# Layernorm stage of a graph layer: the groups overlap on VectorE, tables and weights are moved, two batches are gathered ahead of the barrier

## The reference, cut to what matters

```python
xn = _layernorm(x, axis=-1)                  # x: 6250 x 256, float32
msg = jax.nn.relu(xn[src] + edge_attr)       # 106250 edges, 256 channels
agg = jnp.zeros_like(xn).at[dst].add(msg)    # dst is sorted
h = xn + agg                                 # then an MLP with norms over all nodes
...
qkv = xn @ W_qkv + b_qkv                     # mixing part: q and k centred over channels
attn = v + t2
mix = attn @ W_out + b_out
...
x = x + gnn(xn, ...) + mix
x = x + experts(_layernorm(x))               # top 2 of 8 experts
```

## Time and profile before

| what | us |
|---|---|
| median of 3 runs | 2200.09 |
| lowest and highest run | 2200.0, 2203.48 |
| the profiled execution, its own time | 2199.33 |
| span of the profiled execution | 2197.5 |
| barrier at the end of the layernorm stage (first DVE instruction behind it) | 83.49 |
| last gather of the edge stage issued | 1147.74 |

### The profile page before, as it was taken

One profiled execution on the slowest core, in us unless ns is written; L12 is line 12 of the kernel. 1 busy time (PEld: TensorE's weight loads), 2 busy tenths in 40 slices (PEclk: granted clock), 3 DMA queues, 4 the chain that ended last, 5 costly groups with the idle time before them and its releaser, 6 DMA issues. The chain is left out here.

```text
span 2197.5 us, 33446 instructions
## 1 busy us (share of the span) xinstructions
PE 1781.7 (81%) x10022; PEld 1420.9 (65%) x10023; DVE 1188.2 (54%) x2750; ACT 803.8 (37%) x1624; POOL 1155.5 (53%) x1121
## 2 busy tenths in 40 slices
PE   4267777777778889988886989675899999999996
PEld 3255555555555556655555878564688888888885
DVE  7354554554545555555553767769444544454443
ACT  4133232332323333333322567330344444444443
POOL 1577777777777777777760000220344444444443
PEclk8688888888878898888887999668899999999998
DMA  7566666666666676676652646776123222322332
GB/s 250 184 208 216 214 227 211 219 222 210 225 207 222 220 238 227 225 237 223 226 191 84 220 151 224 203 245 230 36 48 48 43 44 48 48 43 44 48 48 30
DMA packets 142023, 356.34 MB, mean 162 GB/s; under 512 B 33130, under 2 KB 79625, under 8 KB 127611
## 3 DMA queue, kind: packets, MB, share of 16 engines
q0 software_dynamic: 66624, 157.12, 26.9%
q1 hardware_dynamic: 69068, 198.31, 26.2%
q10 hardware_dynamic: 6255, 0.10, 0.3%
HBM read 297.49 MB, written 57.94 MB: 162 GB/s over the span
## 5 line engine op out<-in xcount | busy, mean ns | idle before, releaser
L190 POOL DMA_INDIRECT gathered<-xn_rows,src_table x832 | 821.6, 988 | 260.4 <-issue 252.8
L816 PE MATMUL bank<-edge_attr,dst_select 128*128 128x256 f32 x1664 | 534.0, 492 | 229.0 <-DVE node_sum L642 171.7
L816 PEld LDWEIGHTS bank<-edge_attr,dst_select 128*128 128x128 f32 x1664 | 411.6, 253 | 347.7 <-ACT edge_attr L730 212.2
L630 DVE TENSOR_TENSOR edge_attr<-gathered,edge_attr 128x512 f32<-128x512 f32 x416 | 260.8, 688 | 468.0 <-DMA gathered<-xn_rows,src_table 464.4
L730 ACT ACTIVATE edge_attr<-edge_attr 128x2048 f32<-128x2048 f32 x104 | 198.7, 1910 | 732.7 <-DVE edge_attr L630 732.7
L1797 PE MATMUL bank<-rowsT_parts,expert_weights 128*128 128x256 f16 x3564 | 409.4, 274 | 10.0 <-issue 6.3
L1797 PEld LDWEIGHTS bank<-rowsT_parts,expert_weights 128*128 x3564 | 346.8, 98 | 59.0 <-issue 18.0
L1758 POOL DMA_INDIRECT out<-expert_out,output_row_of_slot x108 | 183.4, 1698 | 301.2 <-ACTq L1856 278.8
L1903 DVE SCALAR_TENSOR_TENSOR gated<-bank,silu 128x512 f32<-128x512 f32 x216 | 120.6, 558 | 184.9 <-ACT silu L1842 173.7
L1810 PE MATMUL bank<-expert_weights,gated_parts 128*128 x1836 | 209.3, 273 | 0.4 <-DVE gated_parts L1911 0.4
L1810 PEld LDWEIGHTS bank<-expert_weights,gated_parts 128*128 128x128 f16 x1836 | 179.5, 98 | 21.5 <-issue 0.7
(11 more groups left out here) (274 smaller groups left out, 1883.4 us busy)
## 6 DMA issues: line engine op xcount, KB each, us to landing
edge_attr<-in_edge_attr SPq DMA_DIRECT2D x104, 1024.0 KB
raw_weights<-in_L_ffn_w SPq DMA_DIRECT2D x32, 544.0 KB, 4.6
expert_weight_parts<-weight_parts SPq DMA_DIRECT2D x32, 544.0 KB, 3.1
expert_weights<-expert_weight_parts SPq DMA_DIRECT2D x8, 2176.0 KB, 24.4
gathered<-xn_rows,src_table POOLq DMA_INDIRECT x832, 3.2
rows_in<-xn_rows SPq DMA_DIRECT2D x48, 128.0 KB
rows_in<-in_x SPq DMA_DIRECT2D x48, 128.0 KB
residual_rows<-key SPq DMA_DIRECT2D x48, 128.0 KB, 2.3
```

The lines of the kernel that those rows point to most:

```text
L190: pool.indirect_dma_start(out=rows[:, e, :], out_offset=None, in_=k.xn_d[:, :], in_offset=bass.IndirectOffsetOnAxis(ap=k.src[:, b, e:e + 1 ...
L630: last = dve.tensor_tensor(ea[:, e:e + ADDED, :], ga[:, e:e + ADDED, :], ea[:, e:e + ADDED, :], ALU.add)
L816: last = pe.matmul(WINP[j % 2][:, 0:C], SEL[j % 3][:, e, :], EA[j % 3][:, e, :], start=e == 0, stop=e == EK - 1)
```

## The change

In the layernorm stage:

- VectorE's `norm` is cut in two. `spread(n)` takes the statistics and merges them; `norm(n)` does the rest. The order is spread(0), spread(1), norm(0), spread(2), norm(1), and so on: the statistics of the next group stand ahead of the normalization of this one.
- Of the tables, only the src table is made between groups: `src_floats` ahead of norm(1), `src_columns` ahead of norm(3). `dst_floats`, `centred`, `bases`, `turned_weights`, `locals_` and `products` follow norm(6).
- TensorE turns the src table behind group 0, and the rest behind group 6.
- ScalarE copies the transposed group n-1 (`turned_rows`) between the square root and the normalization of group n.
- POOL stores all groups, gathers batch 0, waits for the dst table to do its one select, and gathers batch 1, all ahead of the barrier. The loop of the edge stage starts at batch 2.

The number of instructions on VectorE, ScalarE and POOL is as before. The diff, cut to its core:

```diff
@@ scalar
+            for n in range(NG):
+                h = n % 2
+                act.wait_ge(var_done, n + 1)
+                act.activation(std[h][:, :], mv[h][:, :, 1], ACT.Sqrt, bias=k.eps[:, :]).then_inc(std_done, 1)
+                if n >= 1:
+                    turned_rows(n - 1)
+                act.wait_ge(scale_done, n + 1)
+                act.wait_ge(blank, 1)
...
+                last.then_inc(xn_act, 1)
+            turned_rows(NG - 1)
@@ gpsimd
-            for n in range(5):
-                store(n)
-            pool.wait_ge(dst_local, 1)
-            pool.affine_select(out=k.dstl[:, NB - 1, :], in_=k.dstl[:, NB - 1, :], compare_op=ALU.is_ge, fill=0.5,
-                               base=-SEEN, pattern=[[1, EK]], channel_multiplier=EK).then_inc(seen_out, 1)
-            for n in range(5, NG):
+            for n in range(NG):
                 store(n)
             pool.wait_ge(src_ready, 2)
             pool.wait_ge(xn_st, 16 * (NG + 1))
             gather(k, pool, 0, k.GA[0], k.g_in[0])
+            pool.wait_ge(dst_local, 1)
+            pool.affine_select(out=k.dstl[:, NB - 1, :], in_=k.dstl[:, NB - 1, :], compare_op=ALU.is_ge, fill=0.5,
+                               base=-SEEN, pattern=[[1, EK]], channel_multiplier=EK).then_inc(seen_out, 1)
+            gather(k, pool, 1, k.GA[1], k.g_in[1])
@@ vector
-            for n, work in enumerate((None, table_floats, bases, centred, turned_weights, locals_, products)):
+            spread(0)
+            for n in range(NG):
+                if n + 1 < NG:
+                    spread(n + 1)
+                if n == 1:
+                    src_floats()
+                if n == 3:
+                    src_columns()
                 norm(n)
-                if work:
-                    work()
+            for work in (dst_floats, centred, bases, turned_weights, locals_, products):
+                work()
@@ tensor
-            for n, work in enumerate((None, table_turns, base_rows, None, weight_products, None, None)):
+            for n in range(NG):
                 turn(n)
-                if work:
-                    work()
+                if n == 0:
+                    table_turns(srcf, 6, src_turned, 1)
+            table_turns(dstf, 4, dst_turned, 2)
+            base_rows()
+            weight_products()
@@ edge stage, gpsimd
-            for b in range(1, NB):
+            for b in range(2, NB):
```

More of the change, by code:

```diff
@@ L278, in _, with turned_rows @@
             act.wait_ge(k.consts, k.CONST)
[L279 to L289, removed]
+            def turned_rows(n):
                 for s, (g, w) in enumerate(STEPS):
@@ L299, in _ @@
                                        bank[m % BANKS][:, 0:C].rearrange("p (b n) -> p b n", b=CB)[:, :, 0:v], ACT.Copy).then_inc(tr_free, 1)
+            for n in range(NG):
[6 more added lines that the diff above has]
+                act.wait_ge(blank, 1)
+                for g in range(G - ON_ACT, G):
+                    v = valid(n, g)
+                    last = act.activation(k.UTn[0:v, tile(n, g), :], X[n % NX_BUF][0:v, g, :], ACT.Identity,
+                                          scale=rstd[h][0:v, g:g + 1], bias=nmr[h][0:v, g:g + 1])
+                last.then_inc(xn_act, 1)
+            turned_rows(NG - 1)
         @block.gpsimd
@@ L335, in _, with spread @@
             gather(k, pool, 0, k.GA[0], k.g_in[0])
+            pool.wait_ge(dst_local, 1)
+            pool.affine_select(out=k.dstl[:, NB - 1, :], in_=k.dstl[:, NB - 1, :], compare_op=ALU.is_ge, fill=0.5,
+                               base=-SEEN, pattern=[[1, EK]], channel_multiplier=EK).then_inc(seen_out, 1)
+            gather(k, pool, 1, k.GA[1], k.g_in[1])
         @block.vector
         def _(dve):
-            def norm(n):
+            def spread(n):
                 h, x = n % 2, X[n % NX_BUF]
@@ L344, in norm @@
                 dve.drain()
-                if n > 1:
-                    dve.wait_ge(std_done, n - 1)
-                    dve.wait_ge(xn_act, n - 1)
                 for g in range(G):
@@ L351, in norm @@
                 dve.sem_inc(var_done, 1)
+            def norm(n):
+                h, x = n % 2, X[n % NX_BUF]
                 dve.wait_ge(k.consts, k.CONST)
                 dve.wait_ge(std_done, n + 1)
+                if n > 1:
+                    dve.wait_ge(xn_act, n - 1)
                 dve.reciprocal(rstd[h][:, :], std[h][:, :])
@@ L360, in norm, with src_floats, src_columns, dst_floats @@
                 last.then_inc(xn_dve, 1)
-            def table_floats():
+            def src_floats():
                 dve.wait_ge(tab_in, 16 * 6)
+                dve.tensor_copy(srcf[:, :], srci[:, :]).then_inc(tab_f, 1)
+            def src_columns():
+                dve.wait_ge(src_turned, 1)
+                for j in range(2):
+                    dve.tensor_copy(k.src[:, :, 4 * j:4 * j + 4].rearrange("p b k -> p k b"),
+                                    bank[6 + j][:, 0:4 * NB].rearrange("p (k b) -> p k b", k=4)).then_inc(src_ready, 1)
+            def dst_floats():
                 dve.tensor_copy(dstf[:, :], dsti[:, :]).then_inc(tab_f, 1)
-                dve.tensor_copy(srcf[:, :], srci[:, :]).then_inc(tab_f, 1)
             def bases():
@@ L378, in bases @@
                 dve.tensor_copy(basef[0:1, 1, :], basei[0:1, 1, :]).then_inc(base_ready, 1)
[L379 to L382, removed]
             def centred():
@@ L460, in turn, with table_turns @@
                     last.then_inc(tr_full, 1)
[L462 to L468, removed]
+            def table_turns(rows, at, done, count):
+                pe.wait_ge(tab_f, count)
+                for e in range(EK):
+                    last = pe.transpose(bank[at + e // 4][:, (e % 4) * NB:(e % 4 + 1) * NB],
+                                        rows[:, :].rearrange("b (p k) -> b k p", k=EK)[:, e, :], k.ident[0:NB, 0:NB])
+                last.then_inc(done, 1)
             def base_rows():
```

## The result

| | before | after |
|---|---|---|
| median of 20 runs, us | 2204.57 | 2198.48 |
| lowest and highest run | 2199.01, 2208.07 | 2194.81, 2201.46 |
| the profiled execution, its own time | 2199.33 | 2194.86 |
| its first gather | 70.92 | 62.54 |
| its first gather of batch 2 | 95.56 | 86.98 |

The ratio is 0.9976 with a 95% interval of [0.9969, 0.9983]: faster by 5.3 us (3.7 to 6.8); the two medians of the table lie 6.1 us apart. Forecast were 11.0 us. The direction was right, the size twice what came. 2198.48 also lies above the range, partly since the median of before stood at 2204.57 in these runs and not at the 2200.09 I started from; by the ratio, the 2200.09 would have become some 2194.8, inside the range and near rival 2.

The account below looks back on a forecast made before the run. POOL's gather issue sets the edge stage's pace, so the first gather's start counts: 12.8 us earlier, less 0.8 for the select and 1.0 for contention, 11.0 in all. From 2200.1 that gives 2189.1 us, range 2182 to 2196.

Parts of the forecast that it names:

- rival 2: Loads of x as slow as before's median, 8.7 us: 4.2 us later, 2193.3 us; chance 0.16.
- load 3: Layernorm stage, group 3's x: issued at 14.4 behind other loads, 7.0 MB in all, landing at 23.0, read at 23.3.
- load 6: Layernorm stage, last group's x: issued at 35.0 in two pieces, landing at 41.2.
- VectorE's tail: Tables and weights behind the last group, beside POOL's gathers: ends at 79.0, POOL's batch 1 at 79.6.
- the sum: First gather 12.8 us earlier, less 0.8 for the select, less 1.0 for contention: 11.0 us gained.
- the select: Between batches 0 and 1: POOL doesn't wait for the dst table and pays about 0.8 us for select and issue.
- contention: Gathers of batches 0 and 1 slowed by VectorE's work beside them: 1.0 us, bounds 0 and 8.3.
- ScalarE ended 3.0 us behind VectorE: Last group: ScalarE copies group 5's transposes ahead of its tiles, ending at 51.8, VectorE at 48.5.
- Rival 3: Contention at its bound, 8.3 us instead of 1.0: 2196.4 us; chance 0.06.
- rival 4: Gathers move but nothing follows, POOL spending the 11 us in waits on adding: 2199.5 us; chance 0.06.
- rival 1: Loads faster than taken, VectorE the chain throughout: group 6 ends 5.8 us earlier, 2183.3 us; chance 0.14.
- rival 5: Shorter prefetch turns on itself, loads 4 and 6 adding their lateness in full: slower than before, chance 0.03.

Follow-up runs that it names:

- c3: Changed kernel with POOL holding back the stores of groups 3 and 4 until group 6's x has landed; ratio 0.9964.
- d1: Changed kernel with the 106-row piece of x's last load issued as 96 and 10 rows; ratio 0.9908.
- c0: The kernel before, run again unchanged for a second trace; 2200.18 us.
- c1: The changed kernel, run again without edits; 2193.41 us, ratio 0.9971.
- c2: The changed kernel, run once more without edits on the same chip as c1; 2193.40 us, ratio 0.9972.
- b4: Changed kernel with five x buffers, ScalarE's last tiles ahead of group 5's copies, and weights' loads behind all x loads; 2184.25 us, ratio 0.9921.
- b3: Changed kernel with the weights' loads issued behind all loads of x; ratio 0.9954.
- a1: Changed kernel with five buffers for x instead of three, two of them the gather buffers; ratio 0.9934.
- c's chip: The chip shared by the runs c0, c1, c2 and c3; the kernel before took 2200.18 us there.
- d2: Changed kernel with the last store's 106 rows, not the load's, issued as 96 and 10; ratio 0.9951.
- b2: Changed kernel with batch 1 gathered behind the barrier again, leaving only the layernorm stage's change; ratio 0.9996.

## Why the prediction was half right

| step | forecast | after |
|---|---|---|
| load 2 landed | 15.1 | 15.05 |
| norm(1) ended | 20.7 | 20.9 |
| load 3 landed | 23.3 | 24.9 |
| norm(2) ended | 28.0 | 29.9 |
| norm(4) ended | 39.3 | 41.1 |
| load 6: issued, landed | 35.0, 41.2 | 36.6, 45.5 |
| norm(5) ended | 46.0 | 50.5 |
| VectorE, ScalarE done with group 6 | 48.5, 51.8 | 53.0, 56.0 |
| last store issued | 52.4 | 56.6 |
| first gather | 58.1 | 62.5 |
| VectorE's tail, POOL's batch 1 ended | 79.0, 79.6 | 82.0, 83.2 |
| first gather of batch 2 | 82.9 | 87.0 |

**The step that failed** is the landing of the loads, and load 6 above all. Of the 4.4 us at the first gather, 1.6 came from load 3, and 2.6 from load 6, which took 8.9 us where I gave it 6.2. Everything behind, up to the first gather, carried them along nearly unchanged.

For load 3 the rates were near (288 GB/s to 20 us and 355 to 25 us in the changed kernel, against 295 and 374). At these rates the 7.0 MB of the forecast's count would have passed by 23.5 instead of 23.0; by 24.93, when VectorE began on the load, 7.5 MB had. So the larger part of the error is 0.5 MB that the count leaves out. The second store, issued at 21.43, ran beside load 3 and would fill it; no run tests that. For load 6 the choice of row was wrong. The earlier trace rows give the shortest of six loads of 896 KB in one DMA. Load 6 isn't one of them; it is two DMAs, one of 106 rows, and I took a whole load's duration for it, and the shortest at that. The trace of before had the answer in its stretches, which the prediction did not use. Load 6 was issued at 35.27 and 35.69 in it, and the same slow tail stands behind the fast part:

```profile
41.00:42.00 1.00, 0.00 (x0) 0.00 (x0) 0.86 (x7) 0.00 (x0) 0.00 (x0) 1.00 0.86 344
42.00:43.00 1.00, 0.00 (x0) 0.00 (x0) 0.46 (x6) 0.30 (x1) 0.00 (x0) 0.63 0.15 57
43.00:44.00 1.00, 0.00 (x0) 0.00 (x0) 1.00 (x4) 0.83 (x2) 0.00 (x0) 0.50 0.12 50
44.00:45.00 1.00, 0.14 (x1) 0.17 (x2) 1.00 (x4) 0.76 (x2) 0.00 (x0) 0.50 0.09 36
```

It ends near 45, over 9 us behind the issue. It cost nothing then, since VectorE came to group 6 at 59.08; the change took that cover away. With the measured 8.9 us in place of 6.2 the forecast would have been 2189.1 + 2.7 = 2191.8, and with load 3's 1.6 us 2193.4, rival 2's number. Rival 2 named the outcome and gave it 0.16, for another reason (stores beside the loads). c3 and d1 weigh the two reasons, each against runs on its own chip: without stores load 6 takes 7.5 us instead of 9.5 and 9.8, with the 106-row piece cut 5.8 instead of 9.7. The stores are the smaller part, some 2 us against 3.9.

**A second fault lies in the sum.** It takes 0.8 us for the select and 1.0 for contention off the lead, as if POOL had lost nothing there before. But before, three of batch 1's gathers behind the barrier took 1.43 to 1.45 us, and the prediction's own times have batch 2 at 82.9 against 95.56, a lead of 12.7 us, not 11.0. The traces bear the times out: from the first gather to batch 2 the changed kernel took 24.34 to 24.44 us in its four traces, before 24.64 and, in c0, 23.72. What POOL lost on the way by the change was thus between nothing and 0.7 us, not 1.8, and this error hid a part of the other: the lead at batch 2 is 4.1 us short of 12.7, and only 2.4 short of 11.0. What is missing from 11.0 to the 5.3 us measured is 4.4 at the first gather, less 2.0 that POOL did not lose on the way, and 3.3 between batch 2 and the end.

**What held.** ScalarE ended 3.0 us behind VectorE at the last group, as worked out:

```profile
54.47 1.57 ACT L301 ACTIVATE node_sum<-x_in,ln_minus_mean_rstd,ln_rstd 128x256 f32<-128x256 f32 x3
```

- The select and its issue cost 0.4 us (the last gather of batch 0 ended at 72.4, the next began at 72.77), forecast 0.8; 0.3 of it stands between any two gathers. VectorE did wait for it instead:

```profile
72.64 0.59 DVE L419 TENSOR_SCALAR outside_window<-dst_in_window 128x832 f32<-128x832 f32 x1 [6.43 <-POOL dst_in_window L337]
```

- Contention: two gathers of batch 1 took 1.29 us (72.77 and 76.89) instead of 0.95, 0.7 us in all, and the same two took 1.28 to 1.29 in c1, c2 and b4. Each starts within 0.13 us of the start of a TENSOR_SCALAR of VectorE (72.64 and 76.77). I took 1.0; the prediction's estimate by the rule of the Trainium skill, "SBUF — State Buffer", section "Who interferes with whom", was some 2. The trace agrees with the rule in its direction. Rival 3, whose bound for sixteen gathers at 0.5 us is 8.0 and not 8.3, falls.
- The tail and POOL came to the barrier 1.2 us apart, POOL last. It cost 3.8 us, forecast 3.3.
- POOL is the chain of the edge stage; rival 4 falls with b3 and b4, where 9.6 and 17.0 us of lead gave 9.0 and 15.5.
- Loads faster than I took them, rival 1, didn't come with three buffers. With five (a1) VectorE waited 3.1 us for load 3, which landed at 24.25, and for no later one. The estimate of 4.1 us beside it uses a figure that the Trainium skill, "DMA: Bandwidth & Descriptors", section on the anatomy of one DMA, gives for DMAs issued by GpSimd; x's loads are issued by SP, and even with its last piece cut load 6 took 5.8 us (d1).
- The loop of rival 5 did not come: VectorE didn't wait for load 4 at all, and for load 6 4.4 us.

**What stays open.** The pair of the result shows 8.6 us of lead at batch 2 and 5.3 us of gain (3.7 to 6.8). Single executions of one kernel differ by 1 to 2 us at batch 2 (86.98, 87.82, 88.65; before 95.56, 94.72). By the means of these the lead is 7.3 us, and 2.0 us stay unexplained; on c's chip leads of 6.9 and 6.1 and a gain of 6.3 leave nothing. How the run from batch 2 to the last gather comes to vary between 1051 and 1058 us was not settled; the changed kernel alone had 1057.8 and 1052.1.

## What to carry to other kernels

When a change makes an engine faster or takes buffers' slack away, go through the loads one by one with the shape, the queue and the neighbours of each, and look at the bytes per microsecond behind its issue; a load that is late and hidden shows no wait. When the last, odd-sized piece is a load by SP, give most of it a number of rows that spreads over all DMAs, or issue it early; for POOL's store the same cut brought nothing. And look at what a moved piece uncovers: here neither half of the change was worth anything alone.

## What the runs showed of the hardware that I had not expected

- A load of 106 rows of 1 KB at the end of a group left the DMAs busy to a share of 0.14 and less for 2 us (c3; 0.15, 0.12 and 0.09 for 3 us in before). Cut into 96 and 10 rows, the load took 5.8 us instead of 9.7 (d1 and d2).
- At a barrier POOL needs 3.3 to 3.8 us from the end of its last gather to the next one; with VectorE last (b2) it is 0.3 us for VectorE and 0.9 for POOL, from the end of VectorE's work.
- Of the four chips of the experiments two took some 10% longer for the same kernel before (2411 and 2428 against 2200 us), with stretches in which TensorE issued a matmul each 2.1 to 2.8 us. Whether these stretches are all of the difference was not followed.
